# A recurrent chain on one core: TensorE's loop code on registers of its own, its arms jumping straight back to the pair of steps, and one VectorE transposition moved between two subtractions

## What is computed

```
# L0: a plain RNN over time, started from cond
h = tanh(h @ Wh + x_t @ Wx + b);                    x = x + h
# L1: softmax over the two batch rows of <cond, x> / sqrt(512)
x = x + x * softmax_b(cond . x)
# L2: x = x + tanh(x @ W_ih.T + cond @ W_hh.T + b_hh + b_ih)
# L3: a GRU over time, with a "propagation" after every fourth step
z = sigmoid([x_t, h] @ Wz + bz);  r = sigmoid([x_t, h] @ Wr + br)
c = tanh([x_t, r * h] @ Wh + bh); h_new = (1 - z) * h + z * c      # the output
h = tanh(h_new @ Wp + bp) if (t + 1) % 4 == 0 and t < T - 1 else h_new
```

## Time and profile before

| what | value |
|---|---|
| median of 3 runs | 8421.09 us (8420.99 to 8424.03) |
| the profiled execution | 8421.66 us, its span 8419.9 us |
| mean granted TensorE clock | 0.994 |
| PE busy | 8038.6 us, 95% |
| DVE, ACT, POOL busy | 6107.4, 4419.4 and 1877.2 us |
| DMA | 12 GB/s over the span |

### The profile page before, as it was taken

One profiled execution on the slowest core, in us unless ns is written; L12 is line 12 of the kernel. 1 busy time (PEld: TensorE's weight loads), 2 busy tenths in 40 slices (PEclk: granted clock), 3 DMA queues, 4 the chain that ended last, 5 costly groups with the idle time before them and its releaser, 6 DMA issues.

```text
span 8419.9 us, 1113043 instructions
## 1 busy us (share of the span) xinstructions
PE 8038.6 (95%) x504848; PEld 7310.4 (87%) x504848; DVE 6107.4 (73%) x32700; ACT 4419.4 (52%) x26367; POOL 1877.2 (22%) x8458
## 2 busy tenths in 40 slices
PE   6999999999999999999999999999999999999998
PEld 5888888888888888888888888888888888888887
DVE  4777777777777777777777777777777777777776
ACT  2555555555555555555555555555555555555554
POOL 2222222222222222222222222222222222222221
PEclk7999999999999999999999999999999999999999
DMA  1000000000000000000000000000000000000000
GB/s 68 11 10 13 11 10 10 13 11 10 10 13 11 10 10 13 11 10 10 13 11 10 10 13 11 10 10 13 11 10 10 13 11 10 10 13 11 10 11 8
DMA packets 151737, 104.91 MB, mean 12 GB/s; under 512 B 17024, under 2 KB 150528, under 8 KB 150528
## 3 DMA queue, kind: packets, MB, share of 16 engines
q1 hardware_dynamic: 151680, 104.21, 4.0%
HBM read 62.20 MB, written 41.94 MB: 12 GB/s over the span
## 4 chain that ended last, share of the span: by engine, by line
PE 95%; issue 4%; DVE 1%; POOL 0%; ACT 0%; DMA 0%; SPq 0%; POOLq 0%; DVEq 0%
PE ps_c L487 29%; PE ps_r L487 25%; PE ps_l L476 17%; PE ps_z L476 16%; PE ps_mid L454 6%; PE ps_proj L454 2%; PE ps_proj L534 0%; DVE ps_c L660 0%; DVE l_T L656 0%; POOL l_state L379 0%; POOL l_state L383 0%; DMA rnn_h<-w_rnn_h 0%; ACT l_state L838 0%; DVE l_pre L706 0%; DVE rnn_h L693 0%
## 5 line engine op out<-in xcount | busy, mean ns | idle before, releaser
L487 PE MATMUL ps_c<-c_h,rh 128*2 128x64 f32 x131072 | 2251.6, 219 | 5.9 <-issue 5.7
L867 ACT ACTIVATE r_tanh<-ps_r 128x4 f32<-128x4 f32 x4096 | 709.6, 173 | 2663.0 <-DVE ps_r L660 2646.3
L487 PEld LDWEIGHTS ps_c<-c_h,rh 128*2 128x2 f32 x131072 | 1850.6, 84 | 116.1 <-issue 7.5
L476 PE MATMUL ps_l<-rnn_h_parts,l_state 128*6 128x128 bf16 x98304 | 1785.0, 220 | 52.6 <-POOL l_state L383 46.8
L660 DVE STREAM_TRANSPOSE ps_c<-ps_c 128x64 f32<-128x64 f32 x5118 | 1324.4, 262 | 539.7 <-PE ps_c L487 420.8
L660 DVE STREAM_TRANSPOSE ps_r<-ps_r 128x64 f32<-128x64 f32 x4096 | 1084.3, 265 | 870.2 <-PE ps_r L487 842.2
L476 PEld LDWEIGHTS ps_l<-rnn_h_parts,l_state 128*6 128x6 bf16 x98304 | 1500.7, 86 | 64.5 <-ACT ps_l L806 51.1
L487 PEld LDWEIGHTS ps_r<-r_h,h_odd 128*2 128x2 f32 x65536 | 930.0, 85 | 343.8 <-issue 222.1
L379 POOL TENSOR_TENSOR l_state<-l_state 128x8 f32<-128x8 f32 x2048 | 412.7, 201 | 3650.1 <-ACT l_state L838 3648.9
L487 PE MATMUL ps_r<-r_h,h_odd 128*2 128x64 f32 x65536 | 1108.5, 219 | 114.0 <-issue 80.4
L487 PE MATMUL ps_r<-r_h,h_even 128*2 128x64 f32 x65536 | 1143.4, 219 | 11.6 <-DVE h_even L787 8.0
(11 more groups left out here) (98 smaller groups left out, 9683.4 us busy)
## 6 DMA issues: line engine op xcount, KB each, us to landing
gates_spill<-gates_rows SPq DMA_DIRECT2D x128, 192.0 KB, 1.9
gates_seeds<-gates_spill SPq DMA_DIRECT2D x512, 32.0 KB
x_next<-xT SPq DMA_DIRECT2D x128, 64.0 KB, 1.7
x_mid<-xT SPq DMA_DIRECT2D x128, 64.0 KB, 1.7
rnn_spill<-rnn_rows SPq DMA_DIRECT2D x128, 64.0 KB, 1.6
rnn_seeds<-rnn_spill SPq DMA_DIRECT2D x512, 16.0 KB
gates_seeds<-gates_spill SPq DMA_DIRECT2D x512, 16.0 KB
y_out<-y SPq DMA_DIRECT2D x128, 64.0 KB, 1.6
```

The lines of the kernel that those rows point to most:

```text
L476: last = nc.tensor.matmul(psum[QUAD * j:QUAD * j + PARTS * B, 0:P], state_parts(k), w_parts[:, k, j, q, :], start=False, stop=(k == KT - 1 ...
L487: last = nc.tensor.matmul(pair[QUAD * j:QUAD * j + B, n, at:at + W], stationary(k), w[:, k, P * j + W * n:P * j + W * (n + 1)], start=Fals ...
L867: nc.scalar.activation(r_tanh[:, k, :], r_T[n][:, :, 0:B], ACT.Tanh, scale=0.5).then_inc(r_tanh_done[n], 1)
```

## The change

On TensorE, the two nested loops and the `If`s are replaced by labelled blocks and ten registers that the program keeps itself. `even` and `odd` are the numbers of the two steps of a pair, `stop` ends the group, `groups` counts propagations, `chunk` is the projection's chunk, `after_logits`, `after_mid` and `after_gates` are bounds against which `even` is compared, `x_due` and `rows_due` are what the RNN's input waits for. Each arm ends with its own jump to the block of the pair. The products and their order stay as they are, the propagation with its two halves too.

On DVE, the transposition `rnn_T` moves up by one place, between the two subtractions of `split_state`, in all steps where the GRU runs and the RNN is behind.

```diff
-            def pairs_of_steps(g, rnn):
-                start = PROP * g + (AHEAD - PROP)
-                with nc.Fori(start, start + PROP, 2, engines=[pe.engine]) as t:
-                    for u in range(2):
-                        step(rnn, True, t + u, u)
-
-            def projections(g, last):
-
-                chunk = (g >> 2) + LAG
-                with pe.If((g & 2) < 1):
-                    with pe.If((g & 1) < 1):
-                        if last:
-                            pe.nop()
-                        else:
-                            project_rnn_input(chunk + 1)
-                    with pe.Else():
-                        softmax_logits(chunk)
-                with pe.Else():
-                    with pe.If((g & 1) < 1):
-                        project_mid(chunk)
-                    with pe.Else():
-                        project_gates(chunk)
-
-            for first, last in ((LAG, CHUNKS - 2), (CHUNKS - 2, CHUNKS)):
-                with nc.Fori(first_group(first), first_group(last), engines=[pe.engine], head_slot={pe.engine: 0}) as g:
-                    pairs_of_steps(g, True)
-                    propagation(g)
-                    projections(g, last == CHUNKS)
...
+            def pair_of_steps(rnn):
+                step(rnn, True, even, 0)
+                step(rnn, True, odd, 1)
+                pe.reg_add(even, even, 2)
+                pe.reg_add(odd, odd, 2)
+
+            def next_group():
+                pe.reg_add(stop, stop, PROP)
+                pe.reg_add(groups, groups, 1)
+
+            def next_chunk():
+                for register, gain in ((chunk, 1), (after_logits, STEPS), (after_mid, STEPS), (after_gates, STEPS), (x_due, 16), (rows_due, 1)):
+                    pe.reg_add(register, register, gain)
+
+            def chunks(name, last, rnn, rnn_in):
...
+                pe.addr_align(256, offset=0, max_nops=0)
+                pe.br(label("pair"))
+                with arm("pair"):
+                    pair_of_steps(rnn)
+                    pe.br_lt(even, stop, on_true=label("pair"), on_false=label("group"))
+                with arm("group"):
+                    propagation(groups)
+                    pe.br_lt(even, after_mid, on_true=label("early"), on_false=label("late"))
+                with arm("early"):
+                    pe.br_lt(even, after_logits, on_true=label("logits"), on_false=label("mid"))
+                with arm("logits"):
+                    softmax_logits(chunk)
+                    next_group()
+                    pe.br(label("pair"))
+                with arm("mid"):
+                    project_mid(chunk)
+                    next_group()
+                    pe.br(label("pair"))
+                with arm("late"):
+                    pe.br_lt(even, after_gates, on_true=label("gates"), on_false=label("last"))
+                with arm("gates"):
+                    project_gates(chunk)
+                    next_group()
+                    pe.br(label("pair"))
+                with arm("last"):
+                    if rnn_in:
+                        project_rnn_input(None, x_due, rows_due)
+                    next_group()
+                    next_chunk()
+                    pe.br_lt(chunk, last, on_true=label("pair"), on_false=label("done"))
+                nc.switch_bb(label("done"))
...
+            chunks("full", CHUNKS - 2, True, True)
+            chunks("fed", CHUNKS, True, False)
+            chunks("drain", CHUNKS + 1, False, False)
+            last_chunk()
...
                 dve.wait_ge(state_ready[1], t + AHEAD)
                 tt(part(h, 1), part(h, 0), part_top(h, 0), ALU.subtract).then_inc(h_rest_done, 1)
+                if rnn_behind(i, u):
+                    rnn_T(i, u - 1)
                 dve.wait_ge(h_rest_done, t + 1)
                 tt(part(h, 2), part(h, 1), part_top(h, 1), ALU.subtract).then_inc(h_parts_ready, 1)
```

More of the change, by code:

```diff
@@ L614, in _ @@
-            for first, last in ((LAG, CHUNKS - 2), (CHUNKS - 2, CHUNKS)):
-                with nc.Fori(first_group(first), first_group(last), engines=[pe.engine], head_slot={pe.engine: 0}) as g:
-                    pairs_of_steps(g, True)
-                    propagation(g)
-                    projections(g, last == CHUNKS)
[L620 to L626, removed]
-                with pe.If(g < tail + 2):
-                    with pe.If(g < tail + 1):
-                        softmax_logits(CHUNKS)
-                    with pe.Else():
-                        project_mid(CHUNKS)
-                with pe.Else():
-                    with pe.If(g < tail + 3):
-                        project_gates(CHUNKS)
-                    with pe.Else():
-                        pe.nop()
+            names = ("even", "odd", "stop", "groups", "chunk", "after_logits", "after_mid", "after_gates", "x_due", "rows_due")
@@ new lines, in _ @@
+            even, odd, stop, groups, chunk, after_logits, after_mid, after_gates, x_due, rows_due = (pe.alloc_register(n) for n in names)
+            turns = {even: AHEAD, odd: AHEAD + 1, stop: AHEAD + PROP, groups: 1, chunk: LAG, after_logits: AHEAD + PROP + 1,
+                     after_mid: AHEAD + 2 * PROP + 1, after_gates: AHEAD + 3 * PROP + 1, x_due: 16 * (LAG + 3), rows_due: LAG + 2}
+            for register, value in turns.items():
+                pe.reg_mov(register, value)
+            def pair_of_steps(rnn):
[3 more added lines that the diff above has]
+                pe.reg_add(odd, odd, 2)
@@ new lines, in next_group, with label, arm @@
+            def next_group():
[5 more added lines that the diff above has]
+            def chunks(name, last, rnn, rnn_in):
+                def label(part):
+                    return "chunks_" + name + "_" + part
+                def arm(part):
+                    return nc.body(label(part), valid_engines=[pe.engine])
+                pe.addr_align(256, offset=0, max_nops=0)
[29 more added lines that the diff above has]
+                nc.switch_bb(label("done"))
@@ new lines, in last_chunk @@
+            def last_chunk():
+                pe.br("tail_pair")
+                with nc.body("tail_pair", valid_engines=[pe.engine]):
+                    pair_of_steps(False)
+                    pe.br_lt(even, stop, on_true="tail_pair", on_false="tail_group")
+                with nc.body("tail_group", valid_engines=[pe.engine]):
+                    propagation(groups)
+                    next_group()
+                    pe.br_lt(even, STEPS * (CHUNKS + LAG) - PROP, on_true="tail_pair", on_false="tail_end")
+                nc.switch_bb("tail_end")
+                for n in range(2):
+                    pair_of_steps(False)
@@ L728, in iteration @@
                         split_state(i, u)
-                    if rnn_behind(i, u):
+                    if rnn_behind(i, u) and not gru:
                         rnn_T(i, u - 1)
-                        if not gru:
-                            rnn_pre(i, u - 1)
+                        rnn_pre(i, u - 1)
                     if gru:
```

8 lines of the change are left out of this document (3 added, 5 removed).

## The result

The changed kernel takes 8099.07 us (median of 4 runs, 8097.84 to 8100.36), the kernel before 8421.48 on the same chip (4 runs, 8420.99 to 8424.03). The ratio is 0.9617, 95% interval 0.9600 to 0.9633: faster by 322 us where 298 were forecast. The profiled execution took 8099.89 us, its span 8098.1.

The account below looks back on a forecast made before the run. The prediction took PE, 95% busy, plus sequencer control code at loop seams as the bound. Gains of 2.33 us a chunk over 127 chunks, with about 2 us more, made 298 us: 8123 us, range 8085 to 8195.

Parts of the forecast that it names:

- The bound: TensorE's load idle time at loop seams comes from sequencer control code, 4.36 us a chunk; "issue" falls from 4% to about 1%.
- head starts: Control time hidden under the last loads: 0.15 us behind the logits, 0.23 ahead of them, 0.25 at the inner jump back.
- Logits, mid layer, gates: Net gains a chunk from shorter control code around these arms: 0.94, 0.61 and 0.46 us.
- RNN's input: Control code around this arm: gain of 0.05 us a chunk, bounds -0.10 and 0.15, six-way addition taken as 0.15 us.
- RNN's input still near 0.5 and 0.3: Sign in the loads' timeline: idle time around this arm stays near 0.5 us ahead and 0.3 us behind.
- Inner jump back: MOVE and handover go, 0.09 of 0.21 us, counted in three groups of four: 0.27 us a chunk, bounds 0 and 0.36.
- The DVE move: Moving `l_T` between the subtractions costs nothing and gains nothing; c's start stays 0.76 us behind z's.
- 1: Behind the logits, the state's second half holds the whole r product; r's loads over 1.2 us; 8167 us; chance 0.15.
- 2: Sequencer's head start shrinks with the control code, or new blocks carry more; half the gain, 8272 us; chance 0.08.
- 3: More gain: all four inner jumps back, a cheap six-way addition, handovers of 0.04 us; 8076 us; chance 0.09.
- 4: Jumps to the pair from mid-body miss fetched code, 1.70 us each for three arms; slower, 8771 us; chance 0.04.
- 5: z is late on DVE after the move, up to 0.12 us a step; 8369 us; chance 0.04.

Follow-up runs that it names:

- experiments 1 and 2: 1: changed kernel with DVE's old order, 8100.93 us. 2: kernel before with DVE's new order, 8425.61 us against 8424.13.
- Experiment 5: Changed kernel with a register MOVE at the pair's head that the first step's waits read: 8138.89 us.
- experiment 6: Changed kernel with the register additions moved from ahead of the jumps into the stream of products: 8066.23 us.
- experiments 3: Changed kernel with the logits, mid and gates arms leaving through a shared block, one jump more in each: 8123.41 us.
- experiment 7: Kernel with the additions inside the products, plus the two compares that choose the projection moved into the propagation: 8058.78 us.
- experiments 8 and 9: 8: changed kernel with the group's four steps written out, 16472.92 us. 9: whole chunk as straight code with one jump and a prefetch hint, 14867.64 us.

## Why the prediction was right, and where it was off

**The bound.** Right. The idle time was the sequencer's control code: the loads' idle time went where the instructions went, and experiments 1 and 2 put all of the gain on TensorE. "Issue" fell to the 1% forecast. The head starts that the prediction worked out from sums (0.15 us behind the logits, 0.23 behind the propagation, 0.25 at the inner jump) can be read from the trace, as the time from the first control instruction's start to the end of the last load before it: 0.13, 0.22 and 0.25 in the medians, before and after the change.

**Logits, mid layer, gates.** Right: 0.93, 0.55 and 0.50 us net against 0.94, 0.61 and 0.46. As forecast, the logits have no idle time ahead and 0.18 us behind, and r takes 0.96 us instead of 0.90, for the state's second half, for which the 25th load waits (0.154 us against 0.033). The mid layer gave 0.65 before the next r, and what I had left out is that 0.10 comes back: r's loads take 1.00 us behind this arm, I take it because the arm's own products are still running off (no run shows that alone).

**RNN's input: the step that failed.** The prediction has "I count 0.05 us, bounds -0.10 and 0.15", and it was 0.30, outside of its bounds; 0.25 x 124 chunks = 31 us, more than the whole miss of 24. Ahead of the arm it was right in kind (idle time 0.48 to 0.36 in the rows, 0.06 in the medians). Behind it all of 0.34 us went, where the working of the prediction leaves some 0.01. What it had too small is the sequencer's head start behind an arm of 32 wide loads. For the mid layer it got 0.34 as the sum of the instructions behind the `If` less the idle time, and left out that the arm's own jump (L609 there, L601 behind the RNN's input, 0.169 + 0.06) lay under the same loads: 0.34 + 0.23 = 0.57. The rows of the kernel before would have said so: behind both arms this jump starts 0.55 us before the arm's last load ends. With the new list, 0.079 + 0.037 + 0.21 + 3 x 0.06 = 0.51, next to nothing is left in sight, as measured; the six additions at 0.079 in place of the 0.15 assumed are the smaller part. The 0.13 that r then loses behind the arm wasn't counted. So the sign "RNN's input still near 0.5 and 0.3" failed as well: it was 0.36 and nothing.

**Inner jump back.** Right by its price (0.089 to 0.098 a turn against 0.09), and by the count: four jumps gain it, and the logits' group gives one back, since the second half of the state comes late for its third step (its 25th load is 0.232 us behind the 24th, before 0.136). Experiment 5 measured the same MOVE at 0.08, experiment 6 the addition at 0.094.

**The DVE move.** Right at nothing: c starts 0.77 us behind z as before (the earlier trace rows have 0.76), and experiments 1 and 2 show no difference larger than their interval of 0.1 to 0.2%.

**The rivals.** 1: r took 0.96 us and not 1.2, no. 2: the lead did not shrink, no. 3: the cheap addition was so, the handovers stayed at 0.05 to 0.06 (experiments 3 and 5), and 8099 lies between its 8076 and the forecast's 8100 to 8150. Its chance was counted into the range although its 8076 lies below the range's lower end of 8085. 4: not in this change (37 packets in the whole run, jumping compares at 0.20 to 0.21 us), and its price was too small where it does occur: a body past the limit is fetched whole, not once a jump. 5: no.

## What to carry to other kernels

Idle time of the loads at a loop's seams can be costed from the order of the program and the sequencer's rows: each control instruction for its duration and 0.05 to 0.06 us, less a lead that depends on what stands ahead. Read that lead from the rows, separately behind narrow and behind wide products: it is the time from the first control instruction's start to the end of the last load before it. Register additions that can't be removed are cheapest between the matmuls of a product, and jumps behind an arm with many wide loads. A compare within a product costs its time too where a wait stands shortly ahead of it (experiment 7). Before a loop is unrolled to save jumps, count the instructions of its body: here the saving of 0.2 us a jump turned into 1.8 us for every 256 instructions once the body stopped being resident, and the row to look at is the instruction queue's packets.

## What the runs showed of the hardware

- TensorE keeps a loop body of 1745 instructions (37 packets in a whole run, one run) and not one of 2001 (4562 packets). Past the limit each block of 256 instructions costs 1.73 to 1.80 us in all, in straight code too.
- The sequencer's lead over the end of the loads is 0.13 us behind the 8-load arm, 0.22 behind the propagation, 0.25 behind l and 0.55 to 0.57 behind 32 loads of 32 columns. Against the start of a load it is 0.14 us at the propagation's end, nothing 16 loads behind a wait and 0.07 us 16 loads further on (experiment 7).
- Six register additions in one fused operation take 0.079 us, two 0.037. A jump takes 0.169 us, to the end of an `If` (L606 before) as well as back to the pair (L631 after).
- While TensorE waits for code the mean granted clock falls, to 0.894 and 0.959 in experiments 8 and 9 against 0.994: it is at 0.5 (1.2 GHz) for 3503 and 1207 us of them, against 97. In experiment 8 twelve matmuls of z take 0.320 us there and 0.168 at 2.4 GHz, so part of their time is slower products: PE's busy time rose from 7958 to 9465 and 8850 us.
